# Attention with queries and values turned by DMA out of DRAM scratches instead of by TensorE

## The reference

```python
q = (x @ Wq.T + bq).reshape(B, S, H, D)            # H = 32 heads, D = 32; k and v likewise
scores = jnp.einsum('bshd,bsgd->bshg', q, k) * inv_sqrt_d
scores = jnp.where(scores > THRESH, scores, -jnp.inf)
attn = jax.nn.softmax(scores, axis=-1)
out = jnp.einsum('bshg,bsgd->bshd', attn, v).reshape(B, S, Hd)
return out @ Wo.T + bo
...
gate_score = jax.nn.silu(jnp.einsum('bsh,ih->bsi', x, Wg))     # weights dequantised, I = 3584
intermediate = gate_score * jnp.einsum('bsh,ih->bsi', x, Wu)
return jnp.einsum('bsi,hi->bsh', intermediate, Wd)
```

## Time and profile before

| | before |
|---|---|
| median of three executions | 2102.8 us (2102.1 to 2103.78) |
| the profiled execution: its own time | 2104.22 us |
| its span, from the first to the last instruction | 2102.2 us |
| mean granted TensorE clock | 0.994 |
| busy: TensorE / VectorE / ScalarE / GpSimd | 2017.6 / 1592.0 / 1252.8 / 1349.7 us |
| DMA moved | 185.97 MB, of 330006 packets 269168 under 512 B |

### The profile page before, as it was taken

One profiled execution on the slowest core, in us unless ns is written; L12 is line 12 of the kernel. 1 busy time (PEld: TensorE's weight loads), 2 busy tenths in 40 slices (PEclk: granted clock), 3 DMA queues, 4 the chain that ended last, 5 costly groups with the idle time before them and its releaser, 6 DMA issues. The chain is left out here.

```text
span 2102.2 us, 36938 instructions
## 1 busy us (share of the span) xinstructions
PE 2017.6 (96%) x10880; PEld 972.4 (46%) x10880; DVE 1592.0 (76%) x1584; ACT 1252.8 (60%) x2017; POOL 1349.7 (64%) x769
## 2 busy tenths in 40 slices
PE   7899999999998899899999999999999999999997
PEld 5555555555554444334444444444444444444444
DVE  5666766667665300599899989999899989998996
ACT  4578778777775311255666566665656566656653
POOL 1445554645543000058888888888888888888886
PEclk9999999999999999999999999999999999999999
DMA  8363553554454352122122212222112212221208
GB/s 290 91 132 88 106 133 85 113 121 90 111 109 130 101 195 97 30 70 61 45 50 70 60 45 50 53 63 59 48 46 70 60 45 50 68 55 51 50 22 324
DMA packets 330006, 185.97 MB, mean 88 GB/s; under 512 B 269168, under 2 KB 306032, under 8 KB 329968
## 3 DMA queue, kind: packets, MB, share of 16 engines
q1 hardware_dynamic: 329968, 185.46, 34.0%
HBM read 96.29 MB, written 25.17 MB: 58 GB/s over the span
## 5 line engine op out<-in xcount | busy, mean ns | idle before, releaser
L644 PE MATMUL banks<-xt,lower 128*128 128x512 f16 x3584 | 861.7, 379 | 30.0 <-ACT lower L895 16.3
L1212 POOL TENSOR_TENSOR acc<-acc,lower 128x1024 f32<-128x1024 f32 x327 | 772.8, 2368 | 175.2 <-ACT lower L922 175.2
L922 ACT ACTIVATE lower<-banks,down_scale 128x512 f32<-128x512 f32 x654 | 413.8, 683 | 355.9 <-PE banks L669 264.0
L1099 DVE SCALAR_TENSOR_TENSOR lower<-banks,gate_scale,lower 128x1024 f32<-128x1024 f32 x392 | 479.2, 1278 | 146.2 <-PE banks L644 140.2
L644 PEld LDWEIGHTS banks<-xt,lower 128*128 128x128 f16 x3584 | 337.4, 98 | 486.6 <-DVE lower L1099 80.2
L499 PE MATMUL banks<-wt,xt_tile 128*128 128x512 f16 x2304 | 540.0, 380 | 4.2 <-ACT wt L743 2.6
L1099 DVE SCALAR_TENSOR_TENSOR lower<-banks,up_scale,lower 128x1024 f32<-128x1024 f32 x392 | 479.5, 1278 | 51.1 <-PE banks L644 44.9
L669 PE MATMUL banks<-lower 128*128 (+1 forms) x1792 | 458.8, 380 | 5.0 <-DMA lower<-lower 4.4
L1174 POOL TENSOR_TENSOR stacks<-unit,stacks 128x512 f16<-128x512 f32 x192 | 246.7, 1308 | 286.6 <-ACT stacks L768 286.5
L499 PEld LDWEIGHTS banks<-wt,xt_tile 128*128 (+1 forms) x2304 | 215.8, 98 | 220.6 <-issue 4.7
L669 PEld LDWEIGHTS banks<-lower 128*128 (+1 forms) x1792 | 175.2, 98 | 217.6 <-issue 17.3
(11 more groups left out here) (57 smaller groups left out, 1305.8 us busy)
## 6 DMA issues: line engine op xcount, KB each, us to landing
lower<-in_L_ffn_gate_q_dram SPq DMA_DIRECT2D x28, 512.0 KB, 3.7
lower<-in_L_ffn_up_q_dram SPq DMA_DIRECT2D x28, 512.0 KB, 4.5
lower<-in_L_ffn_down_q_dram SPq DMA_DIRECT2D x28, 512.0 KB, 4.1
x_tile<-in_L_attn_x_dram SPq DMA_DIRECT2D x16, 512.0 KB, 3.8
xt_scratch<-xt_tile SPq DMA_DIRECT2D x16, 512.0 KB, 2.8
ctx_scratch<-ctx_parts SPq DMA_DIRECT2D x64, 128.0 KB, 2.1
lower<-ctx_scratch SPq DMA_DIRECT2D x4, 2048.0 KB, 9.2
xt<-xt_scratch SPq DMA_DIRECT2D x4, 2048.0 KB, 15.4
```

The costliest lines, as they stand in the source:

```text
L644: last = mm(psum[:, 2 * (slot % 3) + c, :], gu_t[:, mat, g, :], xt[:, (2 * half + c) * CT:(2 * half + c + 1) * CT, part, g, :], start=(par ...
L922: run(down_tmp[:, buffer, c * BANK:(c + 1) * BANK], psum[:, 6 + c, :], ACT.Copy, scale=scale)\
L1099: v.scalar_tensor_tensor(out=acc_of[:, half, :], in0=gu_pair(slot % 3), scalar=scale[:, :, :].rearrange("p t k -> p (t k)")[:, bass.ds(t * ...
L1212: g.tensor_tensor(acc[:, half, ho, :], acc[:, half, ho, :], down_tmp[:, buffer, :], ALU.add).then_inc(down_added, 1)
```

## The change

Queries and values get DRAM scratches. SyncE stores the finished stack of the queries of tile i as it is (128 rows of 8 KB), waits for the store, and then issues one DMA transpose that reads the scratch as 4096 rows of 128 numbers and writes them as 128 partitions of 4096; likewise the values of tile i - 1. The batches on TensorE and their copies on ScalarE and VectorE go, as do the steps T and R. ScalarE, before it overwrites a stack, waits for its store. In SyncE's order, the values' store is put ahead of the context's, their turn behind the input's; the store and the turn of the queries stand between `store_xt` and the turn of the keys (in the first tile ahead of `store_xt`).

```diff
+    q_dram = nc.dram_tensor("q_scratch", [P, NH * P], F16).ap()
+    v_dram = nc.dram_tensor("v_scratch", [P, NH * P], F16).ap()
...
-        STEPS = [["S0"], ["S1"], ["S2"], ["S3"], ["X"], ["T4"], ["T5"], [], ["T6"], [], ["T7"], [], [], ["R0"],
-                 ["R1"], ["R2"], ["R3", "V0"], ["V1"], [], ["V2"], ["V3"], [], [], []]
+        STEPS = [["S0"], ["S1"], ["S2"], ["S3"], ["X"], [], [], [], [], [], [], [], [], [],
+                 [], [], ["V0"], ["V1"], [], ["V2"], ["V3"], [], [], []]
...
-                    pe.wait_ge(batch_out[0], j * 4 + 2)
-                    pe.wait_ge(batch_out[1], j * 4 + 2)
+                    pe.wait_ge(q_turned, j * 16 + 16)
                     pe.wait_ge(k_turned, j * 16 + 16)
...
-                    pe.wait_ge(batch_out[0], j * 4 + 4)
-                    pe.wait_ge(batch_out[1], j * 4 + 4)
+                    pe.wait_ge(v_turned, j * 16 + 16)
...
-                if u // 2 == K:
-                    wait_pos(act, k_turned, i * 16)
-                elif not isinstance(i, int) or i:
-                    act.wait_ge(batch_done, i * 8 + (2 * (u // 2) - 4))
+                wait_pos(act, (q_stored, k_turned, v_stored)[u // 2], i * 16)
...
+            def store_q(i):
+                sp.wait_ge(unit_lo, i * 6 + (2 * Q + 2))
+                anchor(sp)
+                wait_pos(sp, q_turned, i * 16)
+                anchor(sp)
+                sp.dma_start(q_dram, stacks[:, Q, :, :].rearrange("p x c -> p (x c)")).then_inc(q_stored, 16)
+            def turn_queries(i):
+                if isinstance(i, int) and i == 0:
+                    sp.wait_ge(w_turned, 3 * KT)
+                sp.wait_ge(q_stored, i * 16 + 16)
+                anchor(sp)
+                wait_pos(sp, s_done, i * 4)
+                anchor(sp)
+                sp.dma_start_transpose(turned[:, Q, :], q_dram.rearrange("t (x c) -> (t x) c", c=4 * DH))\
+                    .then_inc(q_turned, 16)
+            def store_v(j):
+                sp.wait_ge(unit_lo, j * 6 + (2 * V + 2))
+                anchor(sp)
+                wait_pos(sp, v_turned, j * 16)
+                anchor(sp)
+                sp.dma_start(v_dram, stacks[:, V, :, :].rearrange("p x c -> p (x c)")).then_inc(v_stored, 16)
+            def turn_v(j):
+                sp.wait_ge(v_stored, j * 16 + 16)
+                anchor(sp)
+                wait_pos(sp, pv_done, j * 4)
+                anchor(sp)
+                sp.dma_start_transpose(turned[:, V, :], v_dram.rearrange("t (x c) -> (t x) c", c=4 * DH))\
+                    .then_inc(v_turned, 16)
...
             def tile_2(i):
                 if not isinstance(i, int) or i + 1 < TT:
                     load_x(i + 1)
+                store_v(i - 1)
                 if not isinstance(i, int) or i > 1:
                     store_context(i - 2)
                 if not isinstance(i, int) or i + 1 < TT:
                     turn_x(i + 1)
+                turn_v(i - 1)
...
                 if projects(i):
+                    store_q(i)
+                    turn_queries(i)
                     turn_k(i)
...
             def first_tile():
                 turn_x(1)
+                store_q(0)
+                turn_queries(0)
                 turn_k(0)
                 store_xt(1)
```

More of the change, by code:

```diff
@@ L165, in build @@
         unit_lo = sem("unit_lo")
+        q_stored = sem("q_stored")
+        q_turned = sem("q_turned")
         k_turned = sem("k_turned")
+        v_stored = sem("v_stored")
+        v_turned = sem("v_turned")
         p_turned = [sem(f"p_turned{k}") for k in range(4)]
-        batch_done = sem("batch_done")
-        batch_out = [sem("batch_out_act"), sem("batch_out_dve")]
         s_done = sem("s_done")
@@ L271, in steps_of @@
                         yield kind, n
-                elif kind == "R":
-                    if projects(i):
-                        yield kind, n
                 else:
@@ L295, in wait_pos @@
                 eng.wait_ge(s, value)
-        BATCH_BANK = 2
         def pair(n):
@@ L311, in weight_pair @@
             return psum[:, n:n + 2, :].rearrange("p b c -> p (b c)")
-        def batch_bank(m):
-            return psum[:, BATCH_BANK + m % 2, :].bitcast(F16)
         def s_pair(k):
@@ L341, in build @@
         k_turns = turned[:, K, :].rearrange("p (x t) -> p x t", t=P)
[L343 to L358, removed]
         FIRST_DOWN = 16
@@ L601, in tile_2 @@
                     for kind, n in steps_of(i, s):
[L602 to L606, removed]
+                        if kind == "S":
                             scores(i - 1, n)
@@ L612, in first_tile @@
                 opening(weights, lambda: None, first_quarter, lambda: None, lambda: None)
-                for m in range(4):
-                    batch(0, m)
             walk(pe, first_tile, tile_2)
@@ L769, in unit_part @@
                 last.then_inc(unit_hi, 1)
[L771 to L774, removed]
             def scores_out(j, k):
@@ L834, in tile_2 @@
                             x_part(i + 1)
[L835 to L838, removed]
                         elif kind == "S":
@@ L863, in first_tile @@
                 opening(weights, lambda: x_part(0), first_quarter, lambda: root(1), lambda: x_part(1))
-                batch_copy(0, 0)
-                batch_copy(0, 2)
             walk(act, first_tile, tile_2)
@@ L994, in unit_copy @@
                                        op0=ALU.mult, op1=ALU.add).then_inc(unit_copied, 1)
[L996 to L999, removed]
             def over_heads(ap):
@@ L1046, in tile_2 @@
                             x_part(i + 1)
[L1047 to L1050, removed]
                         elif kind == "V":
@@ L1081, in first_tile @@
                 opening(weights, lambda: x_part(0), first_quarter, next_norm, lambda: x_part(1))
-                batch_copy(0, 1)
-                batch_copy(0, 3)
             walk(dve, first_tile, tile_2)
```

## The result

The changed kernel takes 2203.4 us (median of five, 2202.97 to 2205.79) against 2102.8 us: 1.048 times the time before, 95% interval 1.0468 to 1.0497. That is 100.6 us slower; forecast were 112 us more, 2215 us, in a range of 2150 to 2300.

A forecast was written before the change was run, and what follows sets the result against it. TensorE bounds the kernel before; after the change SyncE's queue would, with the K turn last. Profiled 2104.2 us + 108 (+7.2 us, 15 times) + 4 for the ends = 2216, beside the median 2215 us; range 2150 to 2300.

The forecast's parts named there:

- Its chain: SyncE's in-order queue per tile, from score step to K turn's landing: period 46.1 us against 38.9, 15 times, +108 us.
- The bound moves from TensorE to the queue: In the attention, TensorE alone would give 34.8 us; the K turn lands at 44.4, so TensorE waits some 7 us.
- The queries' store: On SyncE behind the xt store issued at 27.2 us: both landed at 32.7, with bounds of 30 and 37.
- The turn out of DRAM: The queries' transpose ahead of the K turn, taken at the K turn's 4.8 us; low end 2.7, high end 9.6.
- rival 1: In the attention, turns out of DRAM run at the plain rate: queries 2.7 us, period 44.0, 2183 us; chance 0.17.
- Rival 2: In the attention, turns out of DRAM far slower: at 9.6 us, period +16.0, 2347 us; chance 0.15.
- The clock: After TensorE's wait, the first score steps run at the 1.2 GHz level: +1.6 us a period (0 to 3.1).
- The values' turn in the cover of the softmax: On SyncE behind the x turn: ends at 20.6 us, probabilities' turns start at 21.4, so it fits with 0.8 us cover.
- Rival 3: Faster, if the queries' store and both turns fit ahead of the scores: -2.7 a period at best, 2062; chance 0.08.
- The ends: Opening +2.0; after the last tile context load +2.7, Wo's third load +1, four batches less -1.8; together +3.9 us.
- The sum: Whole kernel: profiled 2104.2 + 108 + 4 = 2216 us; beside the median of 2102.8, 2215 us.
- TensorE's busy time: Sign in the changed kernel's profile: TensorE's busy time down by 50 us or more in spite of the longer span.

The follow-up runs named there:

- the filler: The changed kernel with 24 matmuls, whose results nobody reads, on TensorE ahead of each first score step in tiles that still project: 2179.0 us.
- the run with the values alone: The changed kernel with only the values through the scratch, the queries turned by TensorE in batches as before the change: 2084.6 us.
- the run with both orders mended and the filler on top: The run with both orders mended, plus 10 matmuls whose results nobody reads ahead of the first score step: 2115.6 us.
- the run with both orders mended: The changed kernel with the queries' store issued ahead of the probabilities' turns and the values' turn ahead of the x turn: 2134.8 us.

## Why the prediction was right

Its chain can be laid beside the queue of the changed kernel, in us after the score step at 582.01; the prediction's values are its own terms with the 1.6 us for the clock added.

| | predicted | measured |
|---|---|---|
| x turn issued | 15.7 | 15.7 |
| values' turn issued | 17.4 | 18.0 |
| probabilities' turns issued | 23.0 | 22.9 |
| xt store issued | 28.8 | 28.7 |
| queries' turn issued | 34.5 | 34.2 |
| K turn issued | 39.3 | 38.5 |
| next score step | 46.1 | 45.4 |

- **The bound moves from TensorE to the queue.** Right: the wait of 6.8 us ahead of L493 was forecast as 7, by name of the engine and of the tile.
- **The queries' store**, priced at 5.5 us from the xt store's issue to both landed: right, 5.5 (610.71 to 616.21, the start of the turn behind it).
- **The turn out of DRAM**, taken at the K turn's 4.8 us: mis-sized. It holds the queue for 4.0 us and lands in 6.0 instead of 6.7. While it runs the engines move 290 GB/s, while the K turn runs 215. From its issue to that of the K turn it is 4.3 us, 0.5 less than priced, some 8 us over 15 periods. The answer lies between the forecast and rival 1, which took the plain rate of 385 GB/s and 2.7 us. Rival 2, twice the K turn, is off the table.
- **The clock**, +1.6 us a period: right, and shown alone, 24.4 us by the filler. On the chain it is a little more. The probabilities' turns go out 22.9 us after the score step, in the run with the filler 21.1 (586.24 - 565.18): 1.8 us. That 22.9 meets the 23.0 of the prediction has some luck in it: without the clock they come 1.2 us sooner than before the change (22.3), where 0.9 was forecast.
- **The values' turn in the cover of the softmax**: right. Of its cover of 0.8 us 0.6 is left (it ends at 604.30, the probabilities' turns start at 604.87), and the run with the values alone gains. Where the clock holds, the probabilities' turns go out 21.1 us after the score step both with the values' turn just ahead of them (the filler run) and with it ahead of the x turn (the run with both orders mended and the filler on top, 615.04 - 593.98).
- **Rival 3**, the change pays if store and turns fit: false here, and not to be had by any order tried (2115.6 us at best).
- **The ends**: +2.0 forecast for the opening, measured 81.28 - 79.47 = 1.8: right. For the tail +1.9 was forecast: wrong. What follows the last S0 is 1437.9 us now and was 1439.4, 1.5 less. The context load was to hold up the first output matmul by 2.7 us; it starts 7.1 us after the last S0, as before. What is late there is the first load of Wo. It holds up TensorE ahead of the last S0, until 762.37 and by 8.6 us, but this lies inside the 15th period.
- **The sum**: forecast were 112 us more, the span grew by 99.0. Of the 13 us between, 9.5 are the periods (45.5 instead of 46.1 in the mean) and 3.6 the ends.
- **TensorE's busy time** was to fall by 50 us or more and fell by 23.5. The batches were worth 57 us (1024 matmuls of 56 ns), but a matmul at the lower clock is busy for longer, and the prediction, which had the slow score steps in its sum, left them out of this sign.
- A reading of the earlier trace rows is wrong: GpSimd is busy for 20.94 us of the 40, not 21.6. Nothing hangs on it.
- The Trainium skill's rule that transposing DMAs are as fast as regular ones (Advanced Engine Details and Errata, X-Bar Transpose) doesn't hold for either turn: 215 and 290 GB/s in the stretches above, beside 401 to 442 for the plain store of the queries (612 to 615 us of the changed kernel).
- The Trainium skill's table of the three transpose paths (VectorE: DVE Perf Modes) gives 1309 ns for a bf16 block of 128x128 by DMA. Here, in f16 transfers of 32 blocks, a block held the queue for 150 ns out of SBUF and 125 ns out of DRAM.

What stays open: why a turn out of DRAM is faster than one out of SBUF. The two differ in source and in the order in which they write, and no run here separates these.

## What to carry to other kernels

Work that is taken off the bounding engine is worth its price only where the engine that takes it over isn't on the way to the next start: the same change, a stack turned through DRAM, gained 18 us where its two transfers fell into a queue's idle time and lost some 117 us where they stood ahead of the transfer that releases the next tile. Lay the in-order queue out from one release to the next, with its waits, before moving anything to it; a second transfer laid under one that fills the DMA engines hides its latency but not its bytes. And count what the bounding engine's new idle time does to its clock.

## What the runs showed of the hardware

- The SBUF to SBUF transpose of 1 MB ran at 215 GB/s, the one out of a contiguous DRAM scratch at 290 GB/s, both with the DMA share over 1.1. The issue of either holds SyncE about as long as the data takes (4.87 and 4.0 us; 4.3 for the values), that of a plain 1 MB store 0.36 us. The prediction had priced both turns alike.
- With the 1 MB store under it, the K turn held SyncE for 6.28 us instead of 4.87.
- TensorE's clock fell to the 1.2 GHz level after a wait of 2.4 us for the K turn, in the run with both orders mended, and only once TensorE was at work again (granted clock 1.00 at 571, where the wait ends at 571.92, and 0.50 at 573), while the waits of 1.8 us ahead of V0 left the steps at their old spacing, 1.74 us. 78 us of useless matmuls in the 6.8 us waits made the kernel 24 us faster.
